# Routing gate in plain float32 products instead of split reduced products

## The reference

```python
x = x + gnn(layernorm(x), ...)                  # node and edge work
h = layernorm(x)
logits = h @ gate_w + gate_b                    # [20000, 8]
probs = softmax(logits)
idx = argmax(probs)                             # one expert for each row
# rows are counted through per expert, those past a capacity are dropped
y = (relu(h @ w1[idx] + b1[idx]) @ w2[idx] + b2[idx]) * probs[idx] * kept
out = x + y
```

## Time and profile before

| | before |
|---|---|
| median of 3 runs | 1440.65 us |
| lowest and highest run | 1434.61 and 1442.69 us |
| span of the profiled execution | 1438.1 us |
| its own time beside the span | the profile lists no other time of it; the median lies 2.55 us above its span |
| busy share: TensorE, VectorE, ScalarE, GpSimd | 85%, 70%, 67%, 71% |
| load of the routing stage, first turn to the last logits copy | 368.8 to 471.3 us |
| TensorE clock over the span | 0.931 of full |

### The profile page before, as it was taken

One profiled execution on the slowest core, in us unless ns is written; L12 is line 12 of the kernel. 1 busy time (PEld: TensorE's weight loads), 2 busy tenths in 40 slices (PEclk: granted clock), 3 DMA queues, 4 the chain that ended last, 5 costly groups with the idle time before them and its releaser, 6 DMA issues.

```text
span 1438.1 us, 26842 instructions
## 1 busy us (share of the span) xinstructions
PE 1225.2 (85%) x7872; PEld 1073.0 (75%) x7872; DVE 1006.2 (70%) x2153; ACT 957.1 (67%) x2128; POOL 1022.2 (71%) x920
## 2 busy tenths in 40 slices
PE   2477768888799245999999999999999999999993
PEld 0244444555555135999999999999999999999993
DVE  7999996987799893756657555755755575556652
ACT  4788896886467353767767666766766776667672
POOL 7788688885787105777768766777776777768785
PEclk9977777999899586999999999999999999999997
DMA  9889986453867003433433322423432342233333
GB/s 327 240 265 284 280 203 163 67 75 45 227 214 261 6 10 96 104 47 48 107 47 80 79 45 45 110 44 52 107 48 44 48 110 48 44 49 56 51 54 40
DMA packets 132130, 153.55 MB, mean 107 GB/s; under 512 B 17410, under 2 KB 118850, under 8 KB 131926
## 3 DMA queue, kind: packets, MB, share of 16 engines
q0 software_dynamic: 51648, 64.60, 27.6%
q1 hardware_dynamic: 58758, 66.60, 14.2%
q10 hardware_dynamic: 21648, 21.49, 4.5%
HBM read 98.83 MB, written 53.81 MB: 106 GB/s over the span
## 4 chain that ended last, share of the span: by engine, by line
PE 55%; issue 3%; POOL 2%; ACT 1%; DMA 1%; DVE 0%; ACTq 0%; POOLq 0%; DVEq 0%
PE f_ps_y L1636 27%; PE f_ps_h L1624 26%; PE f_ps_x L1614 2%; POOL out L1515 1%; POOL xg L1497 1%; POOL sg L1501 0%; DMA sg<-stat_rows,idx_row 0%; ACT h_all L1564 0%; ACT h_hi L1563 0%; ACT y_all L1574 0%; ACT f_xn L1548 0%; DMA out<-clean,put_now 0%; DMA sg<-stat_rows,idx_now 0%; DVE clean L1701 0%; DVE x_lo L1669 0%
## 5 line engine op out<-in xcount | busy, mean ns | idle before, releaser
L1563 ACT ACTIVATE h_hi<-f_ps_h,c_b 128x384 fp32r<-128x384 f32 (+1 forms) x416 | 237.1, 570 | 262.9 <-PE f_ps_h L1624 262.9
L1674 DVE TENSOR_TENSOR h_lo<-h_all,h_hi 128x768 fp32r<-128x768 f32 (+1 forms) x208 | 184.2, 886 | 256.6 <-ACT h_all L1564 256.1
L1636 PE MATMUL f_ps_y<-w_hi,h_hi 128*128 128x256 f32 x1136 | 325.2, 286 | 0.0
L1636 PE MATMUL f_ps_y<-w_lo,h_hi 128*128 128x256 f32 x1136 | 320.1, 282 | 0.0
L1636 PE MATMUL f_ps_y<-w_hi,h_lo 128*128 128x256 f32 x1136 | 320.0, 282 | 0.0
L1515 POOL DMA_INDIRECT out<-clean,put_now x159 | 262.8, 1653 | 57.5 <-issue 49.1
L1497 POOL DMA_INDIRECT xg<-out,idx_now x159 | 192.7, 1212 | 128.5 <-issue 118.3
L1624 PE MATMUL f_ps_h<-x_hi,w_hi 128*128 128x384 f32 (+1 forms) x832 | 271.9, 327 | 8.0 <-issue 3.5
L1624 PE MATMUL f_ps_h<-x_lo,w_hi 128*128 128x384 f32 (+1 forms) x832 | 269.3, 324 | 0.0
L1624 PE MATMUL f_ps_h<-x_hi,w_lo 128*128 128x384 f32 (+1 forms) x832 | 269.0, 323 | 0.0
L1564 ACT ACTIVATE h_all<-f_ps_h,c_b 128x384 f32<-128x384 f32 (+1 forms) x416 | 238.1, 572 | 0.0
(11 more groups left out here) (227 smaller groups left out, 2280.7 us busy)
## 6 DMA issues: line engine op xcount, KB each, us to landing
shared<-out SPq DMA_DIRECT2D x40, 512.0 KB, 4.0
w_raw<-in_w SPq DMA_DIRECT2D x16, 1024.0 KB, 7.2
xin<-in_x SPq DMA_DIRECT2D x24, 512.0 KB, 7.0
out<-xin ACTq DMA_DIRECT2D x24, 512.0 KB, 5.2
shared<-in_x SPq DMA_DIRECT2D x16, 512.0 KB, 5.5
out<-shared ACTq DMA_DIRECT2D x16, 512.0 KB, 5.7
dst_row<-in_dst SPq DMA_DIRECT2D x20, 256.0 KB, 4.7
xg<-out,idx_now POOLq DMA_INDIRECT x159
```

The costliest lines, as they stand in the source:

```text
L1563: nc.scalar.activation(h_hi[:, f, :n * P], ps_h[:, f % SLOTS, :n * P], ACT.Relu, bias=b1[:, e, f:f + 1])
L1636: ins = nc.tensor.matmul(ps_y[:, i], x[:, f, i * P:(i + 1) * P], weights[s][:, w], start=i != 1 and f == 0 and n == 0, stop=f == KF - 1 an ...
L1674: tt(h_lo[:, pair, :n * P], h_all[j % 2][:, :, :n * P], h_hi[:, pair, :n * P].bitcast(F32), ALU.subtract).then_inc(h_lo_ready, 1)
```

## The change

The turned rows are copied out once, in plain float32, and multiplied by centred gate weights in plain float32: two products of 512 columns for each group, one for each half of the features. The remainder, the split of the gate weights and the sum of two halves of the logits go. The copies of the logits and the return transposes handle 8 rows instead of 16. GpSimd handles four groups (16 tiles) at a time instead of two.

```diff
-    CG = 2
+    CG = 4
...
-        centred = sb("centred", [P, 2, NEXP])
-        gate_parts = sb("r_gate_parts", [P, 2, 2, NEXP], F32R)
-        raw_logits = sb("raw_logits", [P, NT, 2 * NEXP])
+        gate_centred = sb("r_gate_centred", [P, 2, NEXP])
+        raw_logits = sb("raw_logits", [P, NT, NEXP])
...
-            xt_hi = [load_sb(f"xt_hi{h}", [P, 2, GR], F32R) for h in range(2)]
-            xt_lo = [load_sb(f"xt_lo{h}", [P, 2, GR], F32R) for h in range(2)]
-            lt = [load_sb(f"lt{h}", [2 * NEXP, GR]) for h in range(2)]
+            xt = [load_sb(f"xt{h}", [P, 2, GR]) for h in range(2)]
+            lt = [load_sb(f"lt{h}", [NEXP, GR]) for h in range(2)]
...
             def scaled_logits(n):
                 t = slice(CC * n, CC * (n + 1))
                 pool.wait_ge(logits_taken, CG * (n + 1))
-                chain.link(tt(logits[:, t], raw_logits[:, t, :NEXP], raw_logits[:, t, NEXP:], ALU.add))
-                chain.link(tt(below[:, t], logits[:, t], stat[:, t, 0].unsqueeze(2).broadcast_to([P, CC, NEXP]),
+                chain.link(tt(below[:, t], raw_logits[:, t], stat[:, t, 0].unsqueeze(2).broadcast_to([P, CC, NEXP]),
                               ALU.mult))
...
-                nc.scalar.copy(xt_hi[g % 2][:], ps_t[g % 2]).then_inc(xt_act, 1)
+                nc.scalar.copy(xt[g % 2][:], ps_t[g % 2]).then_inc(xt_ready, 1)
...
                 if g >= 2:
-                    pe.wait_ge(xt_dve, g - 1)
+                    pe.wait_ge(xt_ready, g - 1)
...
             def gate(g):
-                pe.wait_ge(xt_act, g + 1)
+                pe.wait_ge(xt_ready, g + 1)
                 if g >= 2:
                     pe.wait_ge(lt_taken, g - 1)
                 for c in range(2):
-                    nc.tensor.matmul(ps_lt[g % 2], gate_parts[:, c].rearrange("p h e -> p (h e)"),
-                                     xt_hi[g % 2][:, c], start=c == 0, stop=False)
-                pe.wait_ge(xt_dve, g + 1)
-                for c in range(2):
-                    ins = nc.tensor.matmul(ps_lt[g % 2][:NEXP], gate_parts[:, c, 0], xt_lo[g % 2][:, c],
-                                           start=False, stop=c == 1)
+                    ins = nc.tensor.matmul(ps_lt[g % 2], gate_centred[:, c], xt[g % 2][:, c], start=c == 0, stop=c == 1)
                 ins.then_inc(lt_ready, 1)
...
-            def turned_half(g):
-                v.wait_ge(xt_act, g + 1)
-                if g >= 2:
-                    v.wait_ge(lt_ready, g - 1)
-                tt(xt_lo[g % 2][:], ps_t[g % 2], xt_hi[g % 2][:].bitcast(F32), ALU.subtract).then_inc(xt_dve, 1)
...
-            chain.link(tt(centred[:], gate_w[:], ps_mean[:, :NEXP].unsqueeze(1).broadcast_to([P, 2, NEXP]),
-                          ALU.subtract))
-            chain.link(nc.vector.tensor_copy(gate_parts[:, :, 0], centred[:]))
-            tt(gate_parts[:, :, 1], centred[:], gate_parts[:, :, 0].bitcast(F32), ALU.subtract).then_inc(gate_ready, 1)
-            statistics(0)
+            tt(gate_centred[:], gate_w[:], ps_mean[:, :NEXP].unsqueeze(1).broadcast_to([P, 2, NEXP]),
+               ALU.subtract).then_inc(gate_ready, 1)
             for g in range(NG):
-                if g + 1 < NG:
-                    statistics(g + 1)
-                turned_half(g)
+                statistics(g)
```

More of the change, by code:

```diff
@@ L970, in routing_block @@
         ps_l = [banks[:, 4 + h] for h in range(2)]
-        ps_lt = [banks[:2 * NEXP, 6 + h] for h in range(2)]
+        ps_lt = [banks[:NEXP, 6 + h] for h in range(2)]
         ps_mean = banks[:, 7]
@@ L997, in routing_block @@
         lt_taken = sem("lt_taken")
-        xt_act = sem("xt_act")
-        xt_dve = sem("xt_dve")
+        xt_ready = sem("xt_ready")
         logits_ready = sem("logits_ready")
@@ L1108, in take_logits @@
                 nc.scalar.copy(raw_logits[:, GT * g:GT * (g + 1)],
-                               ps_l[g % 2][:, :2 * GT * NEXP].rearrange("p (t e) -> p t e", t=GT)
+                               ps_l[g % 2][:, :GT * NEXP].rearrange("p (t e) -> p t e", t=GT)
                                ).then_inc(logits_taken, 1)
@@ L1165, in turn_back @@
                 for t in range(GT):
-                    ins = nc.tensor.transpose(ps_l[g % 2][:, 2 * NEXP * t:2 * NEXP * (t + 1)],
-                                              lt[g % 2][:, t * P:(t + 1) * P], ident[:2 * NEXP, :2 * NEXP])
+                    ins = nc.tensor.transpose(ps_l[g % 2][:, NEXP * t:NEXP * (t + 1)], lt[g % 2][:, t * P:(t + 1) * P],
+                                              ident[:NEXP, :NEXP])
                 ins.then_inc(logits_ready, 1)
```

## The result

The changed kernel takes 1470.17 us in the median of 4 runs (1467.95 to 1471.97), against 1440.51 of the kernel before: a ratio of 1.0208, with a 95% interval of 1.0182 to 1.0234. The loss is clear of noise; whether it is more than 2% the interval leaves open. The forecast was 1466, in a range of 1458 to 1478, and slower; the measured loss is 29.7 us where the sum gave 25.8. The profiled execution has a span of 1468.3 us and a time of 1470.52.

A forecast was written before the change was run, and what follows sets the result against it. VectorE was taken to bound the routing stage, with TensorE 0.19 us a group behind. Start 0.9, steady part 24.0, last gate 0.8 and end 0.1 summed to +25.8 us, giving 1466 us, range 1458 to 1478.

The forecast's parts named there:

- the sum: Whole kernel: start 0.9, steady part 24.0, last gate 0.8 and end 0.1 make +25.8 us.
- What bounds, and what is hidden: Routing stage: VectorE sets the pace before, TensorE after; then VectorE, ScalarE, row loads and GpSimd's batch are hidden.
- distance of 0.19 us to TensorE: Routing stage before: TensorE's own pace lies 0.19 us a group behind VectorE's, the most that relieving VectorE can give.
- Gate in float32: TensorE's gate products in the routing stage: two float32 products, two records each, cost 1.74 us a group, 0.80 more.
- not slower: Rival on the gate: both products stay under 1.10 us; at 0.96 us, 5.3 us gained, 1435 us; chance 0.03.
- reduced type after all: Rival on the gate: one record per product, ScalarE's 1.8 us the pace, 23 us gained, 1418 us; chance 0.02.
- weight loads not hidden: Rival on the gate: four weight loads a group stand bare, 15 us more, 1481 us; chance 0.06.
- GpSimd late at the end: Rival at the routing stage's end: the last coefficient batch comes late, +4.7 us, 1471 us; chance 0.04.
- The pace: TensorE in the routing load: 0.35 return, 1.74 gate, 0.96 turns, 3.04 us a group; steady part +24.0 us.
- the cover of the weight loads: TensorE in the routing load: four small loads a group hide behind 512-column records and cost nothing.
- the radial product: Edge stage's small float32 product of 512 columns: last record 0.52 us, the upper bound, 2.08 us for four gate records.
- Start and end: Routing stage's ends: first groups at lower clock +0.9 us; last gate +0.8 and GpSimd's operations after the last logits +0.1.

## Why the prediction was right

*What bounds, and what is hidden.* Right. That VectorE set the pace before rests on its unbroken work and the waits on it; no run relieved it alone. (The distance of 0.19 us to TensorE is 2.43 - 2.25 = 0.18 by the rows shown.) Runs show the rest: its relief is worth nothing after (remainder kept: 120.42 us), the loads are not the bound (reduced type: 69.83), and GpSimd's batch hides in the changed kernel, though not in the kernel before, where it costs 1.3 us at the end.

*Gate in float32.* The mechanism is shown: two records a product, 0.43 us apart, 0.86 to 0.87 us a product, and with one product less 31.6 us less. The rivals "not slower", "reduced type after all", "weight loads not hidden" (at its 15 us) and "GpSimd late at the end" are out. The Trainium skill ("FP8 and Floating Point Precision", TensorE Precision Notes) has four passes for a true float32 product; the trace agrees in so far as 0.87 us is 3.7 times the 0.235 us of a reduced product.

*The pace* was mis-sized: 3.04 predicted, 3.18 measured, so the steady part grew by 29.0 us and not by 24.0. What was wrong is the cover of the weight loads, which the prediction cost at nothing: the gate's own small loads are hidden, but those of the turns behind the gate are not. Two terms were off by it. The last of the four gate records costs 0.53 us, not 0.435, and the turns up to the return cost 1.02, not 0.96; with 128 columns, where the load of the turns goes ahead, they are 0.43 and 0.97. The 0.52 us of the radial product in the earlier trace rows, which the prediction set aside as its upper bound because the edge product with 128 columns showed 0.435 back to back, was the right row for that last record: it, too, is the last float32 record, of 64 columns, before something else. That the number of stationary columns does not matter was argued from reduced products; for float32 ones the last record depends on it.

*Start and end.* From the first turn to gate 1 it is 378.07 - 367.33 = 10.74 us, before 8.64: +2.1 where +0.9 was predicted. Of this 1.2 is the second group's rows, which arrived later in this execution (turn 1 starts 4.4 us after turn 0, before 3.2). Between gate 0 and gate 1, where the prediction had its 0.9, it is 0.6: gate 0 took 3.12 us instead of 3.5, as the granted clock rose earlier (0.94 in the window from 376 to 378 us, before 0.77; 0.50 in those ahead of it). The other 0.3 lies between turn 1 and gate 0 (1.86 us, before 1.59, in the reduced type 1.60) and was not foreseen. That the two make 0.9 again is luck. From gate 39 to VectorE's start: 4.26 against 3.63, +0.6 instead of +0.9.

*The sum.* 2.1 + 29.0 + 0.6 = 31.7, less 1.5 us by which the first turn started earlier in this execution, is the 30.2 of the span. VectorE was to start on the logits near 498 and started at 502.75. The median came within 4 us of the forecast, in part by luck: the 1.2 us of the late rows and the 1.5 of the early start nearly cancel, and the range had room for the 5 us that the pace fell short.

## What to carry to other kernels

When a second engine is only 0.2 us a group behind the bound, taking work from the bound is worth 0.2 us at most, and work moved to the second engine is paid in full: count both paces before trading one for the other. Price a product by rows of its own type, and its last record by a row that has something else behind it, not by the middle of a run of equal ones. When an engine waits for a transfer in every step, ask what releases the transfer's buffer before calling memory the bound.

## What the runs showed of the hardware

After a float32 product with 8, 32 or 64 stationary columns the weights of the following transposes were loaded only once the last record had gone through (0.53 us with 8 columns); after one with 128 columns they were loaded 0.43 us earlier, as after reduced products with 8 or 16, where it was 0.23 us earlier. Zeros in 120 more columns thus made the changed kernel's stage 1.7 us faster. The Trainium skill ("TensorE: Matmul & The Clock Gate", Step-by-step: what each phase is for) says that weight loads are pulled ahead of matmuls in flight when their row groups do not conflict or the load goes to a spare weight buffer. For the load of the turns the traces agree behind reduced products and behind 128 float32 columns (0.23 and 0.43 us ahead), and do not behind narrow float32 products. The load of the gate's first record, behind the return transposes, starts with the gate itself in all of these kernels (432.07 us for both in the changed one). Why the cases differ was not settled: the waits between them are not the cause, and whether it is the width itself or how a narrow float32 product is issued stays open.

The first turn of the routing stage started between 362.6 and 370.2 us in the thirteen profiles, with the same edge block. Much of the scatter of whole times between runs comes from there: the changed kernel and its variants with the batch of 8, the remainder kept and the waits moved spread by 6.3 us in whole time, and by 1.3 us when counted from the first turn. So a stretch that begins behind it told differences of 1 us which a whole time could not.
